# Two float32r parts on two halves of the array, and filler planned by key tile, in a macaron block of feed-forward, attention and feed-forward

## The reference

```python
x = x + 0.5 * ffn(layernorm(x))        # base linear + top-2 of 8 LoRA experts of rank 16
x = x + attention(layernorm(x))        # 32 heads of 16, 8 key/value heads, sign weights with row scales
x = x + 0.5 * ffn(layernorm(x))
# inside attention
scores = einsum('bhqd,bhkd->bhqk', q, k) / sqrt(16)
attn = softmax(scores); out = einsum('bhqk,bhkd->bhqd', attn, v)
```

## Time and profile before

| | |
|---|---|
| median of three runs | 1193.02 us (1190.93 to 1193.94) |
| the profiled execution | 1191.72 us, its span 1189.9 us |
| granted clock, mean | 0.972 |
| PE busy | 1078.8 us (91%) |
| DVE busy | 840.7 us (71%) |
| ACT busy | 732.4 us (62%) |
| POOL busy | 282.8 us (24%) |
| DMA | 59.42 MB, mean 50 GB/s |

### The profile page before, as it was taken

The page is one execution under the profiler, slowest core; times in us unless marked ns, Lnnn a source line. Parts: engine busy times, 40 slices in busy tenths (PEclk is TensorE's granted clock), DMA queues, the critical chain, the costliest instruction groups (busy, mean ns, idle before and its releaser), DMA issues.

```text
span 1189.9 us, 16268 instructions
## 1 busy us (share of the span) xinstructions
PE 1078.8 (91%) x5968; PEld 482.1 (41%) x5968; DVE 840.7 (71%) x1146; ACT 732.4 (62%) x1361; POOL 282.8 (24%) x461
## 2 busy tenths in 40 slices
PE   3868687799999999999999999999999999998847
PEld 2656564233423342334333433333333334333335
DVE  3564648777787778787778778878887787773174
ACT  3363733375776677676667676766775676668511
POOL 5034436610241023130032004200500130032010
PEclk9999989699999999999999999999999999999979
DMA  7012132211021102200301131113001200200300
GB/s 247 18 54 85 53 107 91 67 41 43 26 59 30 39 25 63 62 25 26 79 26 26 26 87 30 32 30 77 27 26 49 54 27 26 78 6 6 89 0 36
DMA packets 87360, 59.42 MB, mean 50 GB/s; under 512 B 44145, under 2 KB 73329, under 8 KB 87281
## 3 DMA queue, kind: packets, MB, share of 16 engines
q1 hardware_dynamic: 87280, 58.39, 17.4%
HBM read 37.64 MB, written 20.32 MB: 49 GB/s over the span
## 4 chain that ended last, share of the span: by engine, by line
PE 76%; DVE 10%; ACT 7%; POOL 4%; issue 3%; POOLq 0%; DVEq 0%
PE ps_out L1279 20%; PE ps_score L1267 17%; PE ps_max L1242 16%; PE ps_fill L1200 6%; DVE neg_max L1053 3%; ACT probs L815 2%; PE ps_fill L1227 2%; PE ps_out L1200 2%; PE ps_fill L1185 2%; PE ps_fill L1173 1%; PE ps_fill L1204 1%; PE ps_fill L1217 1%; PE ps_max L1256 1%; ACT xt_h L755 1%; DVE att L1082 1%
## 5 line engine op out<-in xcount | busy, mean ns | idle before, releaser
L815 ACT ACTIVATE probs<-ps_score 128x512 f32<-128x512 f32 x992 | 538.4, 596 | 258.4 <-PE ps_score L1267 257.2
L1053 DVE TENSOR_REDUCE neg_max<-ps_max 128x1 f32<-128x1024 f32 x480 | 572.1, 1220 | 169.9 <-PE ps_max L1242 167.8
L1267 PE MATMUL ps_score<-qst,kst 99*128 99x512 bf16 x992 | 307.4, 385 | 6.3 <-ACT probs L815 4.2
L1242 PE MATMUL ps_max<-kst,qst 96*128 96x512 bf16 x1024 | 290.2, 384 | 15.0 <-DVE neg_max L1111 9.6
L1279 PE MATMUL ps_out<-probs,v_ring 128*32 128x512 f32 x2048 | 273.6, 606 | 3.5 <-ACT probs L815 3.3
L1267 PEld LDWEIGHTS ps_score<-qst,kst 99*128 99x128 bf16 x992 | 77.7, 97 | 263.1 <-ACT probs L815 221.3
L1242 PEld LDWEIGHTS ps_max<-kst,qst 96*128 96x128 bf16 x1024 | 88.6, 98 | 141.5 <-DVE neg_max L1111 19.2
L674 POOL CAST shift<-neg_max 128x16 bf16<-128x16 f32 x32 | 7.1, 221 | 476.3 <-DVE neg_max L1053 476.3
L1279 PEld LDWEIGHTS ps_out<-probs,v_ring 128*32 128x32 f32 x2048 | 40.3, 108 | 96.3 <-issue 87.3
L750 ACT ACTIVATE xn<-xc,ln_shift,rstd 128x512 f32<-128x512 f32 x48 | 38.4, 811 | 47.0 <-POOL ln_shift L585 46.9
L1200 PE MATMUL ps_fill<-wb_h,xt_h 128*128 128x512 f32 x96 | 51.3, 534 | 1.3 <-DVE xc L1040 0.8
(11 more groups left out here) (219 smaller groups left out, 1310.3 us busy)
## 6 DMA issues: line engine op xcount, KB each, us to landing
qst<-q_dram SPq DMA_DIRECT2D x192, 64.0 KB, 2.2
q_dram<-zm SPq DMA_DIRECT2D x24, 256.0 KB, 2.6
kst<-k_dram SPq DMA_DIRECT2D x192, 32.0 KB, 2.2
xc<-x SPq DMA_DIRECT2D x8, 512.0 KB, 4.1
x_dram<-xc SPq DMA_DIRECT2D x8, 512.0 KB, 2.9
xc<-x_dram SPq DMA_DIRECT2D x8, 512.0 KB, 4.4
out<-xc SPq DMA_DIRECT2D x8, 512.0 KB, 3.1
att_dram<-att SPq DMA_DIRECT2D x31, 128.0 KB, 2.2
```

The source lines that it names most:

```text
L815: act.activation(probs[:, kt % 2, j, :], score_bank(i, uu, j), ACT.Exp, scale=1.0 / HD ** 0.5).then_inc(probs_ready, 1)
L1053: dve.tensor_reduce(neg_max[:, uu % 2, t:t + 1], ps_max[max_slot(uu, pos)][:, :, :], AXY, ALU.max, negate=True).then_inc(max_read, 1)
L1242: last = pe.matmul(ps_max[slot][:, half, :], qst[0:SR, r, j, q * P:(q + 1) * P], kst[0:SR, r, half * 512:half * 512 + 512], start=True, st ...
L1267: pe.matmul(score_bank(i, uu, j), kst[0:SR + PARTS, uu, kt * P:(kt + 1) * P], qst[0:SR + PARTS, uu, j, :], start=True, stop=True).then_inc ...
```

## The change

It does several things at once.

- q and k are kept in two float32r parts instead of three bf16 parts. Three products of parts are stacked on 48 rows (`PAIRS` 3, `SR` 48); with the three rows of the shift the scores take rows 0 to 50. The stores and loads move float32 (four bytes) where they moved bf16 (two). `S2` and `S3` are gone.
- The same operands are loaded a second time to rows 64 to 111 for the maxima, which take them from there. Each ring has two units instead of four; `load_for_scores` asks one unit ahead, `load_for_max` three ahead of the scores.
- PE's order in a key tile is score 0, maxima pair, score 1, v products, (turn), score 2, maxima pair, score 3, filler. Before, both pairs stood behind score 3, with filler between them and after them.
- The filler of the loops comes from `FRONT_TILES` and `BACK_TILES`, which give steps by key tile. PE does the steps of key tile k at the end of key tile k; ACT (between exponentials 1 and 2), DVE (between its two reductions), POOL and SP do them in key tile k + 1. What is left at the end of a loop is done there (`flushed`).
- The turn takes the fourth place among a unit's maxima instead of the third (`TURN_POS` 3).
- Raw weights are staged in `v_all` and `o_sb` instead of `qst`.

```diff
-PARTS = 3
-PAIRS = 6
+RING = 2
+PARTS = 2
+PAIRS = 3
 SR = PAIRS * HD
-Q_PARTS = (0, 0, 0, 1, 1, 2)
-K_PARTS = (0, 1, 2, 0, 1, 0)
+TOP = P // 2
+SHIFTS = 3
+Q_PARTS = (0, 0, 1)
+K_PARTS = (0, 1, 0)
...
+BACK_TILES = {
+    6: "T0a T0al", 7: "T0b T0bl", 8: "Oa0", 9: "Oa1", 10: "C0 Ob0", 11: "Ob1", 12: "C1 P0", 14: "P1 ADD",
...
-        qst = sb("qst", [P, UB, REP, BLK], BF16)
-        kst = sb("kst", [P, UB, S], BF16)
+        qst = sb("qst", [P, RING, REP, BLK], F32R)
+        kst = sb("kst", [P, RING, S], F32R)
...
+            def load_for_scores(i, uu):
+
+                if not isinstance(i, int) or UB * i + uu >= RING:
+                    sp.wait_ge(scores_ready, i * (32 * UB) + 32 * (uu - RING + 1))
+                load_qk(i, uu, 0, score_loaded)
+
+            def load_for_max(i, uu):
+
+                if not isinstance(i, int) or UB * i + uu >= RING:
+                    sp.wait_ge(max_scores, max_done(i, uu - RING))
+                load_qk(i, uu, TOP, max_loaded)
...
-                last = pe.matmul(ps_max[slot][:, half, :], qst[0:SR, r, j, q * P:(q + 1) * P],
-                                 kst[0:SR, r, half * 512:half * 512 + 512], start=True, stop=True)
+                last = pe.matmul(ps_max[slot][:, half, :], qst[TOP:TOP + SR, r, j, q * P:(q + 1) * P],
+                                 kst[TOP:TOP + SR, r, half * 512:half * 512 + 512], start=True, stop=True)
...
-                pe.matmul(score_bank(i, uu, j), kst[0:SR + PARTS, uu, kt * P:(kt + 1) * P],
-                          qst[0:SR + PARTS, uu, j, :], start=True, stop=True).then_inc(scores_ready, 1)
+                pe.matmul(score_bank(i, uu, j), kst[0:SR + SHIFTS, uu % RING, kt * P:(kt + 1) * P],
+                          qst[0:SR + SHIFTS, uu % RING, j, :], start=True, stop=True).then_inc(scores_ready, 1)
...
                     score(i, uu, kt, 0)
+                    if kt == 0 and has_max:
+                        pe.wait_ge(max_loaded[uu % RING], i * (UB // RING * LOADS) + LOADS * ((uu + 2) // RING + 1))
+                    for pair in pairs[:1]:
+                        max_matmul(*pair, 0)
+                        max_matmul(*pair, 1)
                     score(i, uu, kt, 1)
...
                     score(i, uu, kt, 2)
-                    score(i, uu, kt, 3)
...
                     for pair in pairs[1:]:
                         max_matmul(*pair, 0)
                         max_matmul(*pair, 1)
-                    for item in plan.get(2 * slot + 1, []):
+                    score(i, uu, kt, 3)
+                    for item in plan.get(slot, []):
                         fill(item)
```

More of the change, by code:

```diff
@@ L247, in macaron @@
         scale_step = sem("scale_step")
-        qk_loaded = [sem(f"qk_loaded{r}") for r in range(UB)]
-        rows_loaded = [sem(f"rows_loaded{r}") for r in range(UB)]
+        score_loaded = [sem(f"score_loaded{r}") for r in range(RING)]
+        max_loaded = [sem(f"max_loaded{r}") for r in range(RING)]
+        rows_loaded = [sem(f"rows_loaded{r}") for r in range(RING)]
         max_scores = sem("max_scores")
@@ L483, in body @@
                     uu, kt = slot // 8, slot % 8
+                    if kt == 0 and not (last and uu == 3):
+                        load_for_scores(i, uu + 1)
                     if kt == 0 and not (last and uu >= 1):
-                        load_qk(i, uu + 3)
+                        load_for_max(i, uu + 3)
                     if kt == 2 and not (last and uu == 3):
@@ L1103, in body @@
                         reduce_pair(i, uu, pos, t)
+                for item in flushed(plan):
+                    fill(item)
             for k, item in enumerate(ALONE):
```

139 lines of the change are left out of this document (61 added, 78 removed), and 8 rows, old and new, of tables (BACK_TILES, FRONT, FRONT_TILES).

## The result

The change made the kernel slower: 1246.53 us median of four runs (1238.97 to 1255.95) against 1193.26 for the kernel before on the same chip, ratio 1.0447 with a 95% interval of 1.0409 to 1.0485. The forecast was 1163 us, with 1212 as the upper end of its range. The profiled run took 1238.97 us, its span was 1237.2 us, and TensorE's mean granted clock was 0.927 where it had been 0.972. It is the fastest of the four runs, so the profile shows the change at its mildest.

A forecast was written before the change was run, and what follows sets the result against it. A key tile costs the larger of the exponential ring (3.10 us) and PE's path with filler (2.42 + F). Fronts -15.2, backs -11.5, last loop +3.0 and start -5 sum to -28.7 on 1191.7: 1163 us, range 1100 to 1212.

The forecast's parts named there:

- Part 1: Maxima beside scores: array halves run fully together, so four matmuls take two streams, 0.47 us instead of 0.94.
- The rival without overlap: Array halves do not run together, so maxima lengthen the key tiles: 134 us more, 1297 us; chance 0.13.
- Part 2: float32r weight loads cost 0.11 us more at two places in a key tile without filler: 2.88 becomes 3.10 us.
- The ring: Dependency loop of v products, score 2, exponentials, score 1 and next v products, setting a key tile without filler: 3.10 us.
- The rival that the loads are hidden: float32r loads proceed while the other half streams; the ring stays 2.88: 56 us less, 1107 us; chance 0.20.
- Part 3: PE's path in key tiles with filler: 2.42 + F, F the filler's PE time, including two mode changes of 0.09 us.
- The sum of a back loop: 32 x 3.10, turns 2.2, v-product copies 0.4, filler and late readers 7.5: 109.4 us against 111.7.
- Part 4: Filler's readers work one key tile later, so PE waits for its one PSUM bank: 0.56 us at RT, 1.3 at Oa0.
- SP's steps move too, and wait only for stores: SyncE's moved steps in the loops were taken to wait for nothing but stores; no cost was given.
- the clock: TensorE's granted clock, read as at its upper level, 1.00, in the earlier kernel's loops; no rival priced a fall.
- The start: Start phase: removed ACT cast and POOL subtraction, and fewer loads before the first maximum: -5 us, bounds -8 and 0.
- The fronts: Two front loops: 109.2 us each against 116.8, -7.6, since more key tiles hold filler and PE's saving shows.

The follow-up runs named there:

- not_beside: halves with both pairs of maxima matmuls behind score 3 and the turn at its old place, so no maximum streams beside a score: 1286.77 us, ratio 1.0776.
- sp_order: ln_behind with SyncE issuing loop 3's first twelve loads ahead of the last chunk's stores and waiting for those at slot 5: 1198.55 us, ratio 1.0034.
- ln_behind: The changed kernel with ScalarE's four LayerNorm steps of a key tile behind exponentials 2 and 3 instead of ahead of them: 1204.73 us, ratio 1.0105.
- sp_wait: The changed kernel with SyncE's four store waits ahead of loop 3 moved to its slot 5: 1259.18 us, ratio 1.0539.
- ln_last_ahead: ln_behind, but in loop 8 alone the LayerNorm steps stand ahead of exponentials 2 and 3 as in the changed kernel: 1236.54 us, ratio 1.0313.
- recover_b: ln_last_ahead with three more matmuls of 128 rows, results unused, in each of key tiles 19 to 23 of loop 8: 1229.02 us, ratio 1.0215.
- clock_fill: ln_last_ahead with nine more matmuls, results unused, behind the filler of key tile 18 in loop 8: 1205.55 us, ratio 1.0082.
- halves: The changed kernel's scores and maxima with the old plan, filler steps in half places in all loops: 1182.91 us, ratio 0.9920 to the kernel before.
- plan_alone: The kernel before (bf16 scores) with the new filler plan in loops 3 to 8 alone: 1199.91 us, ratio 1.0055.
- old_front: halves with the new key-tile plan in loops 3 to 8, the old half-place plan staying in loops 1 and 2: 1210.61 us, ratio 1.0149.
- respaced: halves with four filler steps of loops 3 to 8 moved (second transpose, first two pieces of the attention product): 1174.41 us, ratio 0.9848.

## Why the prediction was wrong

**Right: Part 1.** Full overlap was taken, and not_beside puts 0.47 us on it per key tile with filler. The rival without overlap is refuted by the rows above, where score and maximum start together.

**Right: Part 2.** The ring is 3.09 us against 3.10, and the two places are where the forecast had them: in a key tile of loop 5 score 1 to the v products takes 0.43 us (726.15 to 726.58) where it had 0.32, and score 2 to its exponential 0.53 (727.57 to 728.10) where it had 0.43. The rival that the loads are hidden (1107 us) is refuted; the Trainium skill's rule that it rested on ("TensorE: Matmul & The Clock Gate", Part 3) does not show here across a wait for an exponential.

**Nearly right: Part 3.** Three, six and nine filler matmuls make 3.22, 3.92 and 4.62 us, where 2.42 + F gave 3.12, 3.83 and 4.54. Transitions are 0.1 us dearer, inside their bounds. By the Trainium skill, "TensorEngine Tiling (Array Packing)", Key Properties, they drain the engine; the extra time fits that, though no run takes it apart.

**The sum of a back loop, 109.4.** (32 x 3.10 is 99.2, not the 99.4 of the sum; that is 0.2 us a loop.) The new plan without mishaps gives 111.3 to 111.4 (sp_order, ln_behind). RT's 3.92, Oa0's 4.79 and the FFb pairs came as forecast within 0.1; what was left out were the second transposed tiles (3.29 and 3.72 instead of 3.13) and the key tile behind the third turn, with LayerNorm in it (3.43). They make 1.1 of the 2.0 us that a loop is over; the rest is 0.1 us in each key tile with much filler and 0.06 in each turn. That is 10 us in five loops.

**The step that failed: Part 4**, with the clause "DVE can put its filler off into the rest" beside it and "SP's steps move too, and wait only for stores". I followed late readers through PSUM's bank alone. The step that mattered has no matmul: LayerNorm's statistics moved behind the normalisation on DVE, so POOL and ACT were late, and ACT's place between exponentials 1 and 2 put the exponentials behind that wait. And a wait "only for stores" stood on POOL's split: the last of those stores was issued 2.9 us after loop 3's start, where it had been 3.1 us ahead of it, with twelve loads and the attention rows queued behind, which were asked for 20.8 us after the start instead of 9.5. ln_behind and sp_order remove the two, 41 and 8 us by their ratios. Part 4's own late reader came as forecast: PE waits 1.27 us ahead of Oa0 (1.3 forecast).

**The premise that failed: the clock.** The earlier trace rows showed 1.00 in every loop, and I took it as given for a kernel with other waits. Of the 76 us, by comparing loops with and without the fall, about 16 in the last loop (with the wait that set it off), 8 in loops 4, 5 and 7 and 3 in loop 3 are the low clock; a part of the front loops' and the start's is, too. No rival of mine had it, and this is the largest item. sp_order's profile, without the two mishaps, is still 36 us above the forecast: start +11, front loops +8, back loops +10, last loop +5, end +2.

**The start, −5 forecast.** Among the profiles with the new scores it ended between 231.7 and 246.2 us, most often near 240, where the kernel before had 234.1 (other profiles with the old scores 235.4, 235.4 and 242.2, so a part of this is spread). The casts that went are gone, but the changed kernel's clock was 0.56 in 178 to 234 us instead of 0.81. Filling the time with work didn't pay. What starts the fall there was not found.

**The fronts, 109.2 forecast.** The new plan without the LayerNorm wait needs 114.0 and 112.1 (ln_behind). The mean clock was 0.97 in the first and 1.00 in the second, so most of the 7.7 us is not the clock. In the second the two key tiles with a second transposed tile, at 3.72 each instead of 3.13, make 1.2 of 2.9 us; the rest was not taken apart.

## What to carry to other kernels

When steps move, follow the ones without a matmul too: write down for every engine what stands behind each moved step in program order, and who waits for that. A stall of 1 to 2 us on TensorE is to be priced with the clock that may fall behind it: here one stall of 2.1 us cost 16 us in one kernel and 27 in another, while others of 1.0 to 1.3 us mostly cost only themselves. And separate a change into its parts before judging it: here the scores gained and the plan lost, and the best kernel keeps the first without the second.

## What the runs showed of the hardware

- After 2.09 us without a matmul in loop 8 the granted clock went from 1.00 to 0.50 in all four profiles that have this wait (the changed kernel, sp_wait, ln_last_ahead, recover_b) and stayed there for 38, 61, 61 and 55 us, with PE busy throughout; 2.36 us of useless matmuls in that place kept it at 1.00 (clock_fill). The Trainium skill, "TensorE: Matmul & The Clock Gate", HAM oscillation, tells of the same pattern, waits that make the work after them run at half rate; the trace agrees, with shorter waits than those of its example.
- The length of a wait doesn't decide alone. After the LayerNorm waits of 1.07 to 1.08 us in key tile 17 of the back loops the clock fell in three of five loops of the changed kernel and in all five of sp_wait. After 1.03 us in key tile 7 of halves (six loops), 1.07 us in key tile 16 of plan_alone (five) and 1.27 us in key tile 7 of ln_behind (six) it held, though it fell behind two of the six waits of 1.27 us in the changed kernel; and in old_front it fell twice with no wait above 0.75 us close before. What decides was not found.
- Equal programs differ from run to run: the changed kernel spread over 17 us in four runs, halves over 6, respaced over 13 in six. How much of that is the clock in the loops and how much the start phase was not measured.
- How long the clock stays down differs too. With scores of 51 float32r rows it came back after 3 to 14 us in the back loops (changed kernel, sp_wait), after 38 to 61 us in the part of the last loop that has no maxima, where 15 matmuls of 128 rows in between did not shorten it, and after 58 us in not_beside's first loop. With 99 bf16 rows, in one profile of the last loop, it came back after 4 us. This is not explained.
- Two matmuls on rows 0 to 50 and 64 to 111 start in the same 0.01 us and both last 0.50, as one alone does.
